# Strassen feed-forward: halves of weight pieces written to DRAM in the first pass and read back in the second, two units made during the experts, and a small scatter moved

## The reference, cut to what matters

```python
x = layernorm(x + attention(x))                   # (4, 512, 512) float32, 16 heads
x = layernorm(x + experts(x, itok, ctx_2048))     # 4 experts, one for each token
h = silu(x @ w_gate) * (x @ w_up)                 # (2048 tokens, 512) @ (512, 2048)
h = keep_2_largest_of_4(h)                        # of each group of 4 neighbours, by magnitude
x = layernorm(x + h @ w_down)
```

## Time and profile before

| | us |
|---|---|
| median of 3 runs | 1131.01 |
| the profiled execution, its own time | 1125.83 |
| its span | 1124.1 |
| TensorE busy | 1021.7 (91%) |
| VectorE busy | 889.9 (79%) |
| GpSimd busy | 684.4 (61%) |
| ScalarE busy | 606.6 (54%) |
| experts, from the first transposes to m1(0) | 424.4 to 568.3 |
| feed-forward, m1(0) to the end of m3(31) | 568.3 to 1068 |
| first unit of the second pass, m1(16) | 812.3 |
| what is left (last down products, last norms) | 1068 to 1124.1 |

### The profile page before, as it was taken

One profiled execution on the slowest core, in us unless ns is written; L12 is line 12 of the kernel. 1 busy time (PEld: TensorE's weight loads), 2 busy tenths in 40 slices (PEclk: granted clock), 3 DMA queues, 4 the chain that ended last, 5 costly groups with the idle time before them and its releaser, 6 DMA issues.

```text
span 1124.1 us, 18634 instructions
## 1 busy us (share of the span) xinstructions
PE 1021.7 (91%) x5878; PEld 819.0 (73%) x5879; DVE 889.9 (79%) x1859; ACT 606.6 (54%) x1168; POOL 684.4 (61%) x812
## 2 busy tenths in 40 slices
PE   7989998998999768996989899998989999999985
PEld 6667776776777657775768678877777887777864
DVE  5898699688868975554553898979789798989995
ACT  5787488568848972221345544345344363635524
POOL 2185357446535531444489886959489486989734
PEclk9999999999999998998999899999889999999997
DMA  8877267546725902679424112111021111212101
GB/s 258 239 204 201 68 189 224 150 138 173 208 56 160 281 38 60 78 75 157 69 89 131 38 38 76 38 56 48 10 76 38 51 44 38 75 38 85 57 29 75
DMA packets 63100, 116.80 MB, mean 104 GB/s; under 512 B 8992, under 2 KB 11040, under 8 KB 63008
## 3 DMA queue, kind: packets, MB, share of 16 engines
q1 hardware_dynamic: 58176, 101.49, 35.1%
q0 software_dynamic: 4832, 14.17, 3.4%
HBM read 84.69 MB, written 30.94 MB: 103 GB/s over the span
## 4 chain that ended last, share of the span: by engine, by line
PE 30%; DVE 18%; DMA 5%; issue 5%; ACT 3%; POOL 2%; POOLq 0%; DVEq 0%; ACTq 0%; SPq 0%
PE f_bank L2073 15%; PE f_bank L53 13%; DMA rows<-sorted_dram 5%; DVE beats L2563 2%; DVE h L2603 2%; DVE beats L2571 2%; DVE beats L2573 1%; DVE wins L2582 1%; DVE wd_lo L2617 1%; DVE wins L2584 1%; DVE rows_kept L2624 1%; DVE wins L2585 1%; DVE wins L2589 1%; DVE wins L2590 1%; PE f_bank L2067 1%
## 5 line engine op out<-in xcount | busy, mean ns | idle before, releaser
L714 ACT ACTIVATE probs<-bank,nmax 128x384 f32<-128x384 f32 (+3 forms) x256 | 131.4, 547 | 20.9 <-DVE nmax L899 18.7
L2073 PE MATMUL f_bank<-xb_hi,w_hi 128*128 128x512 f32 x320 | 128.4, 401 | 6.3 <-DVE v L2541 4.4
L883 DVE CUSTOM_DVE_ANT_0 bank<-bank,mask 128x384 f32<-128x384 f32 (+3 forms) x256 | 123.1, 503 | 13.3 <-PE bank L510 12.6
L521 PE MATMUL bank<-ident,probs 128*128 128x128 f32 x640 | 108.7, 284 | 24.4 <-DVE pt_lo L908 10.7
L908 DVE TENSOR_TENSOR pt_lo<-bank,pt_hi 128x512 f16<-128x512 f32 (+1 forms) x192 | 114.9, 598 | 16.6 <-ACT pt_hi L724 16.2
L2073 PE MATMUL f_bank<-xb_lo,w_hi 128*128 128x512 f32 x320 | 126.5, 395 | 0.0
L2073 PE MATMUL f_bank<-xb_hi,w_lo 128*128 128x512 f32 x320 | 126.5, 395 | 0.0
L724 ACT ACTIVATE pt_hi<-bank 128x512 f16<-128x512 f32 (+1 forms) x192 | 104.8, 546 | 23.5 <-PE bank L521 23.0
L53 PE MATMUL bank<-x_hi,w_qk 128*128 128x512 f32 x256 | 101.6, 414 | 7.1 <-DVE x_lo L913 6.6
L53 PE MATMUL f_bank<-wd_hi,hs_hi 128*128 128x512 f32 x224 | 88.5, 395 | 6.9 <-issue 4.7
L521 PEld LDWEIGHTS bank<-ident,probs 128*128 128x128 f32 x640 | 67.1, 141 | 37.7 <-ACT probs L714 23.6
(11 more groups left out here) (311 smaller groups left out, 3033.0 us busy)
## 6 DMA issues: line engine op xcount, KB each, us to landing
big_lo<-q_hi_dram SPq DMA_DIRECT2D x32, 256.0 KB
big_lo<-q_lo_dram SPq DMA_DIRECT2D x32, 256.0 KB
big_lo<-k_hi_dram SPq DMA_DIRECT2D x32, 256.0 KB, 3.7
big_lo<-k_lo_dram SPq DMA_DIRECT2D x32, 256.0 KB, 5.0
gate_raw<-gate SPq DMA_DIRECT2D x32, 256.0 KB
up_raw<-up SPq DMA_DIRECT2D x32, 256.0 KB
wd_raw<-down SPq DMA_DIRECT2D x28, 256.0 KB, 3.7
rows<-sorted_dram SPq DMA_DIRECT2D x19, 256.0 KB
```

The source lines that it names most:

```text
L521: ins = pe.transpose(TP[u % TR][:, j * P:(j + 1) * P], probs[u % RP][:, j * P:(j + 1) * P], ident[:, :])
L714: ins = act.activation(probs[u % RP][:, at:at + cols(r)], S[u % SR][:, at:at + cols(r)], ACT.Exp, bias=nmax[:, r, c:c + 1])
L883: dve.tensor_tensor_reduce(out=S[u % SR][:, at:at + cols(r)], in0=S[u % SR][:, at:at + cols(r)], in1=mask[:, T - cols(r):T], scale=1.0, sc ...
L2073: ins = pe.matmul(out[:, :], (w_hi, w_lo)[a][u % 2][:, w, k, :], piece(x, k)[b], start=(first and n == 0), stop=(n == len(chain) - 1), ski ...
```

## The change

What it does:

- Each unit's pieces are made once, in the first pass. Both halves of the seven pieces (2 x 7 x 128 x 256 x 4 bytes = 1.835 MB for a unit) are written by SyncE to a new DRAM tensor `cut_dram`, in three parts: gates (2 x 256 KB), sums (2 x 384 KB), others (2 x 256 KB).
- In the second pass SyncE reads the same three parts back into `w_hi` and `w_lo`. GpSimd's eight and ScalarE's four instructions for each unit 16 to 31 go, and so do the loads of gate and up for these units.
- Units 5 and 6 are made during the experts (steps 0 to 7), written out at steps 6, 7, 9 and 10, and read back in the first pass, so GpSimd and ScalarE don't make them there.
- In the first pass the load of gate for u waits until the gates of u - 2 have been written out, and ScalarE's rounding of the sums until the sums and others of u - 2 have been written out. SyncE's queue has these writes ahead of the loads.
- The 16 scatters of token numbers (`inverse`) move from the experts' steps 0 to 15 to the groups 16 to 23, two in each, behind `product1`. The load of `order` moves from u = 8 to u = 26, and its wait from group 25 to 26.
- The hardware loop over steps 3 to 10 is written out. The weights of unit 1 are loaded one step later, `x2`'s first block is read three steps earlier, and some waits share a semaphore.

```diff
+        AHEAD_CUT = (5, 6)
+        cut_order = AHEAD_CUT + tuple(u for u in range(MID) if u not in AHEAD_CUT)
+        cut_at = {u: n for n, u in enumerate(cut_order)}
...
+        def comes_back(u):
+
+            return u >= MID or u in AHEAD_CUT
...
-            with eng.Fori(0, (EARLY - 3) // 4) as i:
-                for d in range(3, 7):
-                    step(4 * i + d, d % 4, 1)
-            for n in range(EARLY, NS):
+            for n in range(3, NS):
                 step(n, n % 4, 1 if n < NS - 1 else 2)
...
+            def gate_in(u):
+                if cut_at[u] >= cut_at[2]:
+
+                    sp.wait_ge(s_prod, nth(2, u - 2))
+                if u not in AHEAD_CUT:
+                    sp.wait_ge(s_gate_up_in[u % 2], up_free[u, True])
+                sp.dma_start(m.gate_raw[u % 2][:, :, :], gate[u // J, u % J].rearrange("p (k n) -> p k n", k=KT)).then_inc(s_gate_up_in[u % 2], 16)
...
+            def kept(u, pieces, done):
+
+                for v in range(2):
+                    sp.dma_start(cut_dram[v][u][:, pieces], (w_hi, w_lo)[v][u % 2][:, pieces].bitcast(F32)).then_inc(done[u % 2], 16)
...
+            def others_out(u):
+                sp.wait_ge(s_wl, 4 * cut_at[u] + 4)
+                kept(u, OTHERS, s_cut)
...
+            def gates_in(u):
+                sp.wait_ge(s_prod, nth(2, u - 2))
+                sp.wait_ge(s_gate_up_in[u % 2], up_free[u, False])
+                back(u, GATES, s_gate_up_in)
+
+            def sums_in(u):
+                sp.wait_ge(s_prod, nth(7, u - 2))
+                sp.wait_ge(s_cut[u % 2], cut_free[u, False])
+                back(u, SUMS, s_cut)
+
+            def others_in(u):
+                sp.wait_ge(s_prod, nth(3, u - 2))
+                back(u, OTHERS, s_cut)
...
             for u in range(2, U):
-                weights_in(u)
+                if not comes_back(u - 2):
+                    gates_out(u - 2)
+                    sums_out(u - 2)
+                    others_out(u - 2)
+                if comes_back(u):
+                    gates_in(u)
+                else:
+                    gate_in(u)
+                    up_in(u)
+                if comes_back(u - 1):
+                    others_in(u - 1)
+                if comes_back(u):
+                    sums_in(u)
...
# GpSimd, group(g)
-                up_lo(g)
-                fourth_lo(g)
-                if g + 1 < U:
+                if not comes_back(g):
+                    up_lo(g)
+                    fourth_lo(g)
+                if not comes_back(g + 1):
                     fourth_sum(g + 1)
                     gate_lo(g + 1)
                 if g >= 2:
                     product1(g - 2)
+                if MID <= g < MID + NT // 2:
+                    for t in range(2 * (g - MID), 2 * (g - MID) + 2):
+                        inverse(t)
...
# GpSimd, the experts' step n
                 place(n)
-                if n < NT:
-                    inverse(n)
+                if n in (1, 5):
+                    weight_sums(AHEAD_CUT[n // 5])
+                    fourth_sum(AHEAD_CUT[n // 5])
+                if n in (3, 6):
+                    gate_lo(AHEAD_CUT[n // 6])
+                if n in (4, 7):
+                    u = AHEAD_CUT[n // 7]
+                    sums_lo(u)
+                    up_lo(u)
+                    fourth_lo(u)
...
# TensorE
             def m6(u):
-                pe.wait_ge(s_wl, 4 * u + 2)
+                if comes_back(u):
+                    pe.wait_ge(s_cut[u % 2], cut_landed[u, False])
+                else:
+                    pe.wait_ge(s_wl, 4 * cut_at[u] + 2)
```

More of the change, by code:

```diff
@@ L1553, in late @@
         s_sum, s_wh, s_wl = sem("s_wsum"), sem("s_whi"), sem("s_wlo")
+        s_cut = [sem(f"s_cut{i}") for i in range(2)]
         s_down_in = sem("s_down_in")
@@ L1561, in late @@
         s_x3, s_out = sem("s_x3"), sem("s_fout")
-        s_in = [sem(f"s_x2in{r}") for r in range(NR)]
+        s_in = [sem(f"s_x2in{r}") for r in (0, 1, "s")]
         s_xT, s_xTh, s_xTl = sem("s_x2T"), sem("s_x2Th"), sem("s_x2Tl")
@@ L1565, in late @@
         s_mean, s_sq, s_rs = sem("s_mean"), sem("s_sq"), sem("s_rs")
-        s_order, s_order_in = sem("s_order"), sem("s_order_in")
+        s_order = sem("s_order")
         s_passed = sem("s_late_passed")
         block = ctx.enter_context(nc.Block())
+        AHEAD_CUT = (5, 6)
+        cut_order = AHEAD_CUT + tuple(u for u in range(MID) if u not in AHEAD_CUT)
+        cut_at = {u: n for n, u in enumerate(cut_order)}
+        visits = [(u, True) for u in AHEAD_CUT] + [(u, u < MID and u not in AHEAD_CUT) for u in range(U)]
+        up_free, up_landed, cut_free, cut_landed, up_cut = {}, {}, {}, {}, {}
+        for side in range(2):
+            ups = cuts = 0
+            before = None
+            for u, cut in visits:
+                if u % 2 == side:
+                    up_free[u, cut], cut_free[u, cut] = ups, cuts
+                    up_landed[u, cut], cut_landed[u, cut] = ups + 32, cuts + 64
+                    ups, cuts = ups + (64 if cut else 32), cuts + 64
+                    if cut:
+                        up_cut[u], before = before, cut_at[u]
+        def comes_back(u):
+            return u >= MID or u in AHEAD_CUT
+        GATES, SUMS, OTHERS = slice(G01, G23 + 1), slice(S1, S3 + 1), slice(S4, U23 + 1)
         def later(n, first):
@@ new lines, in up_in, with gates_out @@
+            def up_in(u):
+                if up_cut[u] is not None:
+                    sp.wait_ge(s_wl, 4 * up_cut[u] + 3)
+                sp.dma_start(m.up_raw[u % 2][:, :, :], up[u // J, u % J].rearrange("p (k n) -> p k n", k=KT)).then_inc(s_gate_up_in[u % 2], 16)
+            def kept(u, pieces, done):
+                for v in range(2):
+                    sp.dma_start(cut_dram[v][u][:, pieces], (w_hi, w_lo)[v][u % 2][:, pieces].bitcast(F32)).then_inc(done[u % 2], 16)
+            def gates_out(u):
+                sp.wait_ge(s_wl, 4 * cut_at[u] + 1)
+                kept(u, GATES, s_gate_up_in)
@@ new lines, in sums_out, with back @@
+            def sums_out(u):
+                sp.wait_ge(s_wl, 4 * cut_at[u] + 2)
+                kept(u, SUMS, s_cut)
+            def others_out(u):
+                sp.wait_ge(s_wl, 4 * cut_at[u] + 4)
+                kept(u, OTHERS, s_cut)
+            def back(u, pieces, done):
+                for v in range(2):
+                    sp.dma_start((w_hi, w_lo)[v][u % 2][:, pieces].bitcast(F32), cut_dram[v][u % MID][:, pieces]).then_inc(done[u % 2], 16)
+            def gates_in(u):
+                sp.wait_ge(s_prod, nth(2, u - 2))
+                sp.wait_ge(s_gate_up_in[u % 2], up_free[u, False])
+                back(u, GATES, s_gate_up_in)
@@ L2118, in m4 @@
             def m4(u):
-                pe.wait_ge(s_wl, 4 * u + 3)
+                if not comes_back(u):
+                    pe.wait_ge(s_wl, 4 * cut_at[u] + 3)
                 pe.wait_ge(s_copy, 3 * u + 3)
@@ L2124, in m3 @@
             def m3(u):
-                pe.wait_ge(s_wl, 4 * u + 4)
+                if not comes_back(u):
+                    pe.wait_ge(s_wl, 4 * cut_at[u] + 4)
                 pe.wait_ge(s_sum_up, c22_count(u))
@@ L2225, in step @@
                                ACT.Copy).then_inc(s_gh, 1)
+                if isinstance(n, int) and n in (3, 6):
+                    gate_hi(AHEAD_CUT[n // 6])
+                if isinstance(n, int) and n in (4, 7):
+                    u = AHEAD_CUT[n // 7]
+                    sums_hi(u)
+                    up_hi(u)
+                    fourth_hi(u)
                 if isinstance(n, int) and n == EARLY + 2:
@@ L2821, in build @@
         late(nc, big_at, x2, context, ident, tile_expert, slot_idx, place_idx, sorted_rows, s_sc, ordered_rows, order_dram,
-             gate, up, down.rearrange("(c p j) n -> c p j n", p=P, j=4), out.rearrange("b t d -> (b t) d"),
+             cut_dram, gate, up, down.rearrange("(c p j) n -> c p j n", p=P, j=4), out.rearrange("b t d -> (b t) d"),
              N, E, D, I)
```

99 lines of the change are left out of this document (56 added, 43 removed).

## The result

The changed kernel takes **1096.18 us** (median of 4 runs, 1094.46 to 1100.11) where the kernel before takes 1130.05 beside it: a ratio of 0.9704, 95% interval 0.9662 to 0.9747. On another chip it was 1093.80 against 1127.28. So -34 us, where -12 was predicted (1119, range 1086 to 1142). By the profiled executions it is 1124.1 - 1095.5 = 28.6 us of span; the rest of the difference is that the profiled execution of before (1125.83 us by its own time) was faster than its four timed runs here (1126.55 to 1133.93).

A forecast was written before the change was run, and what follows sets the result against it. TensorE's own pace was taken to bound most of the second pass, with waits for VectorE elsewhere and the experts slowed by scatters holding DMA engines. -18 - 5 - 11 - 6 + 28 = -12, so 1131 - 12 = 1119 us, range 1086 to 1142.

The forecast's parts named there:

- The experts: Experts' 17 steps: scatters leave, 2 us taken back for new work and writes; -18 us, bounds 0 and -19.8.
- The first pass: First pass: GpSimd skips units 5 and 6, VectorE's 4.43 us wait cut to about 2; -5 us, bounds 0 and -6.5.
- The middle: From 773 to 845 us: GpSimd no longer makes units 16 and 17, VectorE speeds up; -11 us, bounds 0 and -15.
- The rest of the second pass: Second pass after its first units: only 7 us not TensorE's own pace; -6 us, ends 0 and -7.
- Reading back: Second pass: loads of the kept halves land just in time, others_in(u) tightest; 0 us, up to +5.
- The queue didn't fill: Rival, groups 16 to 23: 16 scatters at 9 us plus transfers make the stage DMA's; 1146 us, slower, chance 0.17.
- VectorE was freed: Rival claimed the opposite: VectorE's slow instructions not due to GpSimd, or new transfers take GpSimd's place; 1141 us, chance 0.07.
- no collision: Rival, second pass: moved scatters hold nobody there; -40 us, 1091 us, chance 0.28.
- the signs named: Steps 6.4 to 6.9 us, VectorE's row near 1.25, waits at m6(18), m6(21), m6(22), high DMA share at low GB/s.
- The scatters, moved: +28: Groups 17, 20, 21: moved scatters delay loads by 7.6, 3.4 and 10 us, plus clock; +28 us, ends 0 and +55.
- two in a row hold the engines for 15 us: Second pass: a scatter priced at 7.5 us on the slowest engine, so a pair holds from m1 + 6 to m1 + 21.
- The clock's part: Second pass: slower granted clock behind two of the waits made by moved scatters, 2 x 3.4 us within the +28.

The follow-up runs named there:

- experiments 1, 2 and 7: Changed kernel, scatters back in the experts: 1105.12 us; kernel before, scatters alone moved: 1107.06 us; kernel before, nothing moved, scatters writing 512-byte rows: 1108.46 us.
- experiment 4: Changed kernel without units 5 and 6 made ahead during the experts: 1103.54 us, ratio 0.9807.
- experiment 5: Changed kernel with five unneeded GpSimd subtractions a group added in groups 16 to 29: 1110.80 us, ratio 0.9846.
- experiment 6: Changed kernel with the same 16 scatters in the same places, each writing rows of 512 bytes: 1083.15 us, ratio 0.9623.
- experiment 9: Changed kernel, 4-byte scatters to places 512, 64, 16 bytes apart: 1086.43, 1083.61, 1084.63 us; 256-byte rows: 1084.70; kernel before, places 512 apart: 1107.48.
- experiment 3: The changed kernel run again, unedited, beside other runs on the same chip: 1093.80 us, ratio 0.9684.
- experiment 11: Changed kernel with one scatter a group in groups 8 to 23 in place of two in 16 to 23: 1102.04 us, ratio 0.9787.

## Why the prediction was right or wrong

**Right:** the direction, and that the scatters are what holds the engines (experiments 1, 2 and 7). The experts: -18 by the text, -20.3 in the profile; the 2 us taken back for the new writes weren't owed, and experiment 4 shows the two units to cost nothing there. The first pass: -5 by the text, -8.2 measured. Its wait at unit 5 was rightly put down to VectorE (experiment 4), but taken as cut to 2 us where it went. The middle: -11, measured -7.6, for one of its waits stayed (4.9 us for `rows_kept`); that it was VectorE that was freed there is argued from what the waits were for, not shown. The rest of the second pass: -6, measured -7.5, all there was; experiment 5 brings about as much back with work for GpSimd alone. Reading back: 0, and 0 it is (experiment 6).

**The rivals and the signs.** No rival of the text came true as a mechanism. The queue didn't fill: that rival took 9 us of held engines a scatter and said itself that it needs 6 on average, where the experts' rows give 2.6 (experiment 9). Its 9 us "behind one scatter" are read from 506 to 518, in which two are issued (505.9 and 512.3). VectorE was freed. The time, 1096, lies nearest to the 1091 of "no collision", though the collisions were there: the other parts gave some 4 us more than forecast and the collisions took half. Of the signs named, the steps (110.7 / 17 = 6.5 us), VectorE's row (1279 ns) and the waits for what is read back came as said; the DMA share over 0.8 did not come with few GB/s (0.95 at 256 in 868 to 879).

**Wrong: the term "The scatters, moved: +28".** The profile shows 15.1 (some 10 in the profile of experiment 3), and that is 13 of the 16.6 us by which the sum missed the span. The mechanism and its places were right, the size not.

The step that failed is "two in a row hold the engines for 15 us", twice a price of 7.5. Two scatters don't add up: a pair has landed 11.6 us after its first issue, one alone after 9.4 (experiment 11), so from the time at which a scatter reaches the engines, 1.6 us behind its issue as the text estimated it, a pair holds them for some 10 us. In group 17 the pair has landed 15.7 us after m1(17), in group 21 16.7 us after m1(21), where the text held the engines until m1 + 21. All three places were less late for it. m6(18) waited 4.3 us where 7.6 was forecast, m6(21) 1.0 where 3.4, and `others_in(22)` came 4.1 us after m6(22) would have been due, and 2.2 in experiment 3, where the text had 10. The clock's part, 2 x 3.4 in the sum, is 0.07 x 10 + 0.09 x 11 + 0.16 x 22 = 5.2 by the windows; with the waits of 4.3, 1.0 and 4.2 that makes 14.7 of the 15.1. The 3.4 was too much for its own place as well: group 5 lost 7.3 us before, of which 4.4 are the wait.

The text also overlooked a path that changed little here. In the first profile the down weights, 14 us on the way, held ScalarE's queue and with it the copy `v`, so that m4(21) waited 4.2 us, about as long as m6(22) would have. The text had the down weights in the queue, and asked only what they delay there, not who waits for them.

**Why a scatter costs what it does** was read too simply, without a change to the sum. The text took the held engines as fitting a rule of the Trainium skill ("DMA: Bandwidth & Descriptors", Specifications), that below 512 bytes the engine does a read-modify-write. Experiment 9 lands the same 4 bytes in 2.6 us, so size below 512 bytes doesn't by itself hold an engine here; whether a read-modify-write is part of what neighbours do to each other, no run shows. The same page's price for one DMA from GpSimd (Anatomy of one DMA, a fixed 2.0 us or so), which the text set aside, fits a scatter to places apart, whose fastest landing is 2.1. The trace of before couldn't have told size from distance, since it has one kind of scatter only; but the text didn't name the question.

**The best of the runs** is the changed kernel with its places 64 bytes apart (1083.61, 0.9609), beside the rows of 512 and 256 bytes (0.9623 and 0.9617); their intervals overlap. Against the changed kernel's own 0.9704 and 0.9684 that is another 0.8 to 1.0%, 10 to 13 us, for one constant in the routing and a longer tensor in DRAM.

## What to carry to other kernels

When DMA engines show a high share and few bytes, look for the transfer that holds them before moving work around it (0.68 at 75 GB/s was such a mark, 0.80 at 288 GB/s was not); here making it cheap (one factor on an index) gave as much as moving it, and together with the move it took away the collisions too. A scatter of single numbers into neighbouring places took three times as long to land here as one into places 16 bytes or more apart, and the loads beside it came late too. When a transfer comes late, follow every engine that waits for it, and what stands behind that wait in its queue.

## What was unexpected of the hardware

- 128 writes of 4 bytes by one indirect DMA land in 8.7 us (median) where the places are 4 bytes apart, in 3.0 at 16 bytes, 2.6 at 64 and 512; 128 writes of 512 bytes take 2.6 to 2.7. Only distances of 4, 16, 64 and 512 were tried, and why neighbours hold each other up no run shows.
- While such a scatter is on its way, other DMAs land late too: loads of 256 KB in 10.2 us in the experts, against 2.6 beside scatters at a distance. On average an engine is busy 2.6 us longer for a scatter there, but single packets of 2048 bytes take up to 6.9 us, where the longest beside scatters at a distance takes 0.64.
- Two such scatters issued 1.3 to 1.6 us apart have landed 11.6 us after the first issue (median), one alone after 9.4: they overlap for the most part.
